# Attention on one core: four column groups of the P·V sums gathered by DMA and added on GpSimd, in place of a closing product on TensorE

## The reference

```python
ctx = X @ We.T
influence = jnp.einsum('bqe,bke->bqk', ctx, ctx)
...
Q, K, V = (heads(Wq), heads(Wk), heads(Wv))
scores = jnp.einsum('bhqd,bhkd->bhqk', Q, K) * SCALE + 0.1 * influence[:, None]
attn = jax.nn.softmax(scores, axis=-1)
out = jnp.einsum('bhqk,bhkd->bhqd', attn, V)
out = out.transpose(0, 2, 1, 3).reshape(b, s, d) @ Wo.T
```

## Time and profile before

| what | value |
|---|---|
| median of 3 runs | 4101.06 us (4098.67 to 4104.31) |
| the profiled execution's own time | 4091.76 us |
| its span, first to last instruction | 4090.0 us |
| mean granted TensorE clock | 0.968 of full speed |
| busy: PE, DVE, ACT, POOL | 93%, 81%, 61%, 12% |
| attention | first product at 483.0 us, last store issued at 3733.3 us of the span |

### The profile page before, as it was taken

How to read it: one execution, slowest core, us unless ns; L and a number is a source line. 1 busy time by engine, 2 the same in 40 slices (tenths; PEclk the granted TensorE clock), 3 DMA queues, 4 the chain that set the end, 5 groups by cost and what they waited for, 6 DMA issues and landing times. The chain is left out here.

```text
span 4090.0 us, 91456 instructions
## 1 busy us (share of the span) xinstructions
PE 3806.7 (93%) x29214; PEld 2212.5 (54%) x29214; DVE 3301.8 (81%) x5171; ACT 2483.3 (61%) x2892; POOL 472.8 (12%) x272
## 2 busy tenths in 40 slices
PE   1997599999999999999999999999999999995698
PEld 1786445555554555555555555555555555553587
DVE  7995488888888888788888888888888888885797
ACT  2663256666666666666666666666666666663464
POOL 3882100000000000000000000000000000000487
PEclk6998799999999999999999999999999999997899
DMA  3002611212122122212121212121212121213200
GB/s 122 1 0 84 160 35 36 44 37 45 36 47 41 41 40 42 44 36 44 36 44 38 44 39 44 38 44 36 44 36 45 38 45 37 47 38 92 69 18 20
DMA packets 316656, 186.52 MB, mean 46 GB/s; under 512 B 195447, under 2 KB 246551, under 8 KB 315831
## 3 DMA queue, kind: packets, MB, share of 16 engines
q1 hardware_dynamic: 316342, 182.35, 20.1%
HBM read 147.75 MB, written 33.82 MB: 44 GB/s over the span
## 5 line engine op out<-in xcount | busy, mean ns | idle before, releaser
L1164 DVE TENSOR_REDUCE tops<-coarse 128x1 f32<-128x512 f32 x4144 | 2681.3, 686 | 578.6 <-PE coarse L1025 475.2
L1140 ACT ACTIVATE probs<-fine 128x1024 f32<-128x1024 f32 x2048 | 1998.5, 1022 | 1014.9 <-PE fine L1044 1014.8
L1055 PE MATMUL o_ps<-probs,vh 128*32 128x512 f32 x8192 | 1088.9, 604 | 0.2 <-ACT probs L1140 0.2
L1034 PE MATMUL fine<-query_a,key_a 64*128 64x512 f32 x4096 | 921.1, 446 | 23.1 <-issue 19.6
L1034 PEld LDWEIGHTS fine<-query_a,key_a 64*128 64x128 f32 x4096 | 386.4, 185 | 929.1 <-ACT probs L1140 750.6
L1025 PE MATMUL coarse<-key_a,max_query 64*128 64x512 f32 x4144 | 832.6, 397 | 43.2 <-DMA key_c<-scratch_c_key 22.3
L1044 PE MATMUL fine<-query_b,key_b 33*128 33x512 f32 x4096 | 816.5, 394 | 0.0
L1040 PE MATMUL fine<-query_c,key_c 64*128 64x512 f32 x4096 | 814.5, 393 | 0.0
L1025 PEld LDWEIGHTS coarse<-key_a,max_query 64*128 64x128 f32 x4144 | 394.2, 186 | 113.5 <-DVE tops L1164 30.0
L1044 PEld LDWEIGHTS fine<-query_b,key_b 33*128 33x128 f32 x4096 | 388.9, 185 | 88.8
L1040 PEld LDWEIGHTS fine<-query_c,key_c 64*128 64x128 f32 x4096 | 389.3, 186 | 82.9
(11 more groups left out here) (158 smaller groups left out, 2377.3 us busy)
## 6 DMA issues: line engine op xcount, KB each, us to landing
query_c<-scratch_c_query SPq DMA_DIRECT2D x258, 128.0 KB, 2.6
max_query<-scratch_q_hi SPq DMA_DIRECT2D x524, 32.0 KB, 1.8
max_query<-scratch_c_query SPq DMA_DIRECT2D x262, 64.0 KB, 2.0
query_a<-scratch_q_hi SPq DMA_DIRECT2D x516, 32.0 KB, 1.8
query_a<-scratch_c_query SPq DMA_DIRECT2D x258, 64.0 KB, 2.0
query_b<-neg_max SPq DMA_DIRECT2D x1032, 0.5 KB, 2.0
query_b<-scratch_q_lo SPq DMA_DIRECT2D x258, 32.0 KB, 2.4
scratch_attended<-result SPq DMA_DIRECT2D x512, 8.0 KB
```

Source lines behind the costliest of these rows:

```text
L1034: pe.matmul(fine[i % 2][:, r, :], key_a[kp][half_rows(r, 0, HALF), cols], query_a[half][half_rows(r, 0, HALF), :], start=True, stop=False)
L1055: last = pe.matmul(o_ps[32 * j:32 * (j + 1), :], vh[kp][:, kt, :], probs[:, kt // 2 % RING, kt % 2, :], start=g == 0, stop=g == NG - 1)
L1140: act.activation(probs[:, i % RING, :, :], fine[i % 2][:, :, :], ACT.Exp).then_inc(probs_ready, 1)
L1164: dve.tensor_reduce(tops[n][:, idx // KB, idx % KB:idx % KB + 1], bank[:, :], AX.X, ALU.max).then_inc(tops_ready, 1)
```

## The change

`finish`, `take_result` and the bank `o_fin` go. ACT copies `o_ps` to one of two `ot` buffers. SP issues four SBUF-to-SBUF DMAs (`gather`) that put the four groups, 17 rows each, side by side on 17 partitions as `part`. POOL adds them in two instructions (`add_parts`): 17 x 1024, then 17 x 512. SP stores `result` with 2 DMAs instead of 5, now behind `load_max`. The ring's skip after unit 23 stays as it is, under the name `SKIP_AFTER`, with nothing in the skipped bank.

```diff
-FINISH_AFTER = 23
+SKIP_AFTER = 23
 SUMS_AFTER = 1
-RESULT_AFTER = 2
...
-        ot = sb("ot", [P, QB])
+        ot = [sb(f"ot{n}", [P, QB]) for n in range(2)]
+        part = [sb(f"part{n}", [DK + 1, QT, QB]) for n in range(2)]
...
-        result = [sb(f"result{n}", [P, P]) for n in range(2)]
+        result = [sb(f"result{n}", [DK + 1, QB]) for n in range(2)]
...
-        o_fin = coarse[(FINISH_AFTER + 1) % COARSE][:, 0:P]
...
+                def add_parts(u, n):
+
+                    pool.wait_ge(gathered[n], G_LEAD + GATHERS * (u + 1))
+                    pool.wait_ge(stored[n], R_LEAD + STORES * u)
+                    pool.tensor_tensor(part[n][:, 0:2, :], part[n][:, 0:2, :], part[n][:, 2:4, :], ALU.add).then_inc(sum_chain, 1)
+                    pool.wait_ge(sum_chain, 2 * u + n + 1)
+                    pool.tensor_tensor(result[n][:, :], part[n][:, 0, :], part[n][:, 1, :], ALU.add).then_inc(result_ready, 1)
...
                 with pool.Fori(0, H // 2 - 1) as hp:
                     for n in range(2):
+                        add_head(2 * hp + n)
 
                         pool.wait_ge(pv_done, V_LEAD + NG * NQB * (2 * hp + n + 1))
                         load_v(n, 2 * hp + n + 2)
...
+                def gather(s, n):
+
+                    sp.wait_ge(ot_ready, O_LEAD + s + 1)
+                    for j in range(QT):
+                        sp.dma_start(part[n][:, j, :], ot[n][32 * j:32 * j + DK + 1, :]).then_inc(gathered[n], 16)
+
                 def store(s, n):
 
-                    sp.wait_ge(result_ready, N_LEAD + s + 1)
+                    sp.wait_ge(result_ready, s + 1)
                     s = (s + STEPS) % STEPS
-                    for j in range(QT):
-                        sp.dma_start(scratch["attended"][bass.ds(s // NQB * DK, DK), bass.ds(s % NQB * QB + j * P, P)],
-                                     result[n][32 * j:32 * j + DK, :]).then_inc(stored[n], 16)
-                    sp.dma_start(scratch["sums"][bass.ds(s // NQB, 1), bass.ds(s % NQB * QB, QB)].rearrange("h (j t) -> (h j) t", j=QT),
-                                 result[n][DK:P:32, :]).then_inc(stored[n], 16)
+                    sp.dma_start(scratch["attended"][bass.ds(s // NQB * DK, DK), bass.ds(s % NQB * QB, QB)], result[n][0:DK, :]).then_inc(stored[n], 16)
+                    sp.dma_start(scratch["sums"][bass.ds(s // NQB, 1), bass.ds(s % NQB * QB, QB)], result[n][DK:DK + 1, :]).then_inc(stored[n], 16)
...
+                                unless_start(half, kp, hp, i, lambda: gather(s - 1, 1 - half))
                                 load_max(s + 1, 1 - half)
+                                unless_start(half, kp, hp, i, lambda: store(s - 1, 1 - half))
...
+                gather(STEPS - 1, 1)
                 store(STEPS - 1, 1)
...
-                        if i == FINISH_AFTER + COARSE:
-                            pe.wait_ge(result_ready, t)
-                        elif not isinstance(t, int) or t > 0 or i >= COARSE:
-                            behind = COARSE if i <= FINISH_AFTER or i > FINISH_AFTER + COARSE else COARSE - 1
+                        if i != SKIP_AFTER + COARSE and (not isinstance(t, int) or t > 0 or i >= COARSE):
+                            behind = COARSE if i <= SKIP_AFTER or i > SKIP_AFTER + COARSE else COARSE - 1
                             pe.wait_ge(tops_ready, UNITS * t + i - behind + 1)
...
-                def finish(s, free):
-
-                    pe.wait_ge(ot_ready, O_LEAD + s + 1)
-                    pe.wait_ge(tops_ready, free)
-                    for j in range(QT):
-                        last = pe.matmul(o_fin[32 * j:32 * (j + 1), :], sel[:, :], ot[:, j * P:(j + 1) * P], start=True, stop=True)
-                    last.then_inc(fin_ready, 1)
...
-                            if unit + 1 == FINISH_AFTER:
-                                before(lambda: finish(s - 1, UNITS * (s + 1) + FINISH_AFTER + 2 - COARSE))
                             times_v(s, kp, i // GROUP - 1)
...
-                def take_sums(s):
+                def take_sums(s, n, earlier):
 
                     act.wait_ge(pv_done, V_LEAD + NG * (s + 1))
-                    act.wait_ge(fin_ready, F_LEAD + s)
-                    act.activation(ot[:, :], o_ps[:, :], ACT.Copy).then_inc(ot_ready, 1)
-
-                def take_result(s, n, earlier):
-
-                    act.wait_ge(fin_ready, F_LEAD + s + 1)
-                    act.wait_ge(stored[n], R_LEAD + STORES * earlier)
-                    act.activation(result[n][:, :], o_fin, ACT.Copy).then_inc(result_ready, 1)
...
+                    act.wait_ge(gathered[n], G_LEAD + GATHERS * earlier)
+                    act.activation(ot[n][:, :], o_ps[:, :], ACT.Copy).then_inc(ot_ready, 1)
```

More of the change, by code:

```diff
@@ L849, in attention_phase @@
         coarse_ready, tops_ready, neg_ready = sem("coarse_ready"), sem("tops_ready"), sem("neg_ready")
-        ot_ready, fin_ready, result_ready = sem("ot_ready"), sem("fin_ready"), sem("result_ready")
+        ot_ready, sum_chain, result_ready = sem("ot_ready"), sem("sum_chain"), sem("result_ready")
+        gathered = [sem(f"gathered{n}") for n in range(2)]
         stored = [sem(f"stored{n}") for n in range(2)]
-        P_LEAD, V_LEAD, F_LEAD, N_LEAD, O_LEAD = 2, RING // GROUP, 1, 1, 1
-        STORES = 16 * (QT + 1)
-        R_LEAD = 2 * STORES
+        P_LEAD, V_LEAD, O_LEAD = 2, RING // GROUP, 1
+        STORES, GATHERS = 16 * 2, 16 * QT
+        R_LEAD, G_LEAD = 2 * STORES, 2 * GATHERS
         C_DMAS, K_DMAS, KB_DMAS, Q_DMAS, MQ_DMAS, M_DMAS = 16 * 6, 16 * 4, 16 * 2, 16 * 10, 16 * 6, 16 * 2 * QT
@@ L890, in load_v, with add_head @@
                     pool.tensor_copy(vh[n][:, :, 0:DK], v_all[:, head, :, :]).then_inc(v_ready, 1)
+                def add_parts(u, n):
[4 more added lines that the diff above has]
+                    pool.tensor_tensor(result[n][:, :], part[n][:, 0, :], part[n][:, 1, :], ALU.add).then_inc(result_ready, 1)
+                def add_head(head):
+                    with pool.Fori(0, NQB // 2) as i:
+                        for n in range(2):
+                            add_parts(head * (NQB // 2) + i, n)
                 load_v(0, 0)
@@ L895, in _ @@
                     for n in range(2):
+                        add_head(2 * hp + n)
                         pool.wait_ge(pv_done, V_LEAD + NG * NQB * (2 * hp + n + 1))
                         load_v(n, 2 * hp + n + 2)
+                for head in range(H - 2, H):
+                    add_head(head)
             @block.sync
@@ L1016, in max_scores @@
                     for i in (idx, idx + 1):
[L1017 to L1020 removed]
+                        if i != SKIP_AFTER + COARSE and (not isinstance(t, int) or t > 0 or i >= COARSE):
+                            behind = COARSE if i <= SKIP_AFTER or i > SKIP_AFTER + COARSE else COARSE - 1
                             pe.wait_ge(tops_ready, UNITS * t + i - behind + 1)
                     for i in (idx, idx + 1):
[L1023 removed]
+                        bank = coarse[(i if i <= SKIP_AFTER else i + 1) % COARSE]
                         q, r, kb = i // KB, i % 2, i % KB // 2
@@ L1142, in body @@
                             if unless_first is None:
-                                take_sums(s - 1)
+                                take_sums(s - 1, 1 - half, u + half - 1)
                             else:
                                 with act.If(unless_first):
-                                    take_sums(s - 1)
-                        if i == RESULT_AFTER:
-                            if unless_first is None:
-                                take_result(s - 1, 1 - half, u + half - 1)
-                            else:
-                                with act.If(unless_first):
-                                    take_result(s - 1, 1 - half, u + half - 1)
+                                    take_sums(s - 1, 1 - half, u + half - 1)
                 steps(act, body)
-                take_sums(STEPS - 1)
-                take_result(STEPS - 1, 1, STEPS // 2 - 1)
+                take_sums(STEPS - 1, 1, STEPS // 2 - 1)
             @block.vector
@@ L1162, in reduce_max @@
                         dve.wait_ge(coarse_ready, UNITS // 2 * t + idx // 2 + 1)
-                    bank = coarse[(idx if idx <= FINISH_AFTER else idx + 1) % COARSE]
+                    bank = coarse[(idx if idx <= SKIP_AFTER else idx + 1) % COARSE]
                     dve.tensor_reduce(tops[n][:, idx // KB, idx % KB:idx % KB + 1], bank[:, :], AX.X, ALU.max).then_inc(tops_ready, 1)
```

18 lines of the change are left out of this document (8 added, 10 removed).

## The result

The changed kernel takes 4113.91 us in the median (4110.38 to 4117.25, 7 runs), the kernel before 4101.06 us (4091.66 to 4104.52, 7 runs). The ratio is 1.0032, 95% interval 1.0020 to 1.0044. The forecast was 4101, range 4085 to 4112. The profiled execution took 4110.38 us with a span of 4108.6 us, 18.6 us longer than that of before. (The profile of before is at the fast end of its runs, 4091.76; the difference of the medians is 12.9.)

What follows compares the result with a forecast made beforehand. PE was taken to set the pace. -6 us in the loop and +5.7 in the tail made 0 within rounding: 4091.5 for the profiled execution, and 4101 with the 9.3 us by which the median lies above it; range 4085 to 4112.

Steps and rivals of the forecast that it cites:

- the wait for unit 23 takes the closing product's place: PE, each step: units 24 and 25 still wait for DVE, so removal gains only 0.047 us, 6 us in all; chance 0.70.
- the product's whole 0.25 us: PE, each step: rival that the wait does not bind, gaining 0.25 us a step, 32 us, to 4075; chance 0.08.
- The load is exposed: PE's weight load for units 24 and 25: no longer hidden, so the product follows 0.34 us after it, not 0.23.
- POOL does not slow DVE's reductions: POOL's adds beside DVE's reductions in the attention: cost taken as 0; the rival, POOL holds DVE, 4470 us, chance 0.04.
- The adds' sum: POOL's two adds a step: 2.43 and 1.21 us, 3.6 us together.
- ACT's lighter load: ACT in the attention: the result's copy goes, worth nothing because ACT waits for PE in most pairs.
- SP's queue: SP's DMAs inside the loop: stores behind load_max push the max_query loads by about 1.2 us, at no cost.
- The tail: Behind the last step: gather, adds and stores without cover take 9.6 us against 3.95, costing 5.7 us, bounds 3.9 and 8.
- lands 2.0 us later: In the tail: the gather's fourth issue begins at about +1.3 us and lands 2.0 us later, at +3.3.
- What is removed on PE: PE without the closing product: it then waits 0.34 us for DVE, gaining 0.047 us a step, 6 us in all.
- longer fetch of code at a loop's end: At a loop's end: a slower outcome given no size, sharing a chance of 0.08 with the longer tail.
- the tail grows: Behind the last step: rival of a 4 us gather or falling clock, 4110 to 4115; 0.08 shared with longer code fetch.

Runs made afterwards that it cites:

- half reductions: Changed kernel with DVE reducing only the first 256 of 512 columns of units 22 and 23: 4085.59 us, ratio 0.9968 to the kernel before.
- the shifts: Changed kernel with 64, 128 or 192 more PE instructions (tiny unused products) once ahead of the attention's first products: 4125.86, 4104.57 and 4105.04 us.
- the 48: Kernel before with 48 more PE instructions (12 tiny products) ahead of the attention's first products, none of the change: 4115.09 us, ratio 1.0040.
- the shift by 128: Changed kernel with 128 more PE instructions (tiny unused products) once ahead of the attention's first products: 4104.57 us, ratio 1.0019 to the kernel before.

## Why the prediction was wrong

**Right.** The step that the wait for unit 23 takes the closing product's place: 0.047 us a step forecast, 0.04 measured (from the early units of the second group to the fourth group's first product 6.00 us, where 6.01 were forecast and 6.06 stood before), the product's whole 0.25 us only with the wait gone (half reductions). The load is exposed, as read from step 0. POOL does not slow DVE's reductions (686 ns). The adds' sum holds, with a little luck, as the first is 0.05 us shorter and the second 0.07 longer than forecast. ACT's lighter load shows no gain: PE's wait accounts for the whole of a step's 0.04 us. SP's queue: later than forecast, since the stores also wait for the adds, but of no cost in a plain step; made as late in the kernel before it cost nothing either.

**The first step that failed: "The tail", its term "lands 2.0 us later".** The mechanism was right, the size was not: 5.7 us forecast, 10.8 measured between marks (10.2 on SP's queue). From the gather's first issue to its use it is 8.34 us for 3.3. With 32 rows it is 3.92, so 4.4 of the 5.0 us are the 17 rows, and 0.6 is the rest, the slower issues among it. I took the landing time from a DMA of another shape, of 0.5 KB, and so missed that the number of rows decides over how many DMA engines a transfer spreads. The Trainium skill ("DMA: Bandwidth & Descriptors", section Why a DMA increments its semaphore by 16 and not by 1) says that a DMA uses the largest number of engines, up to 16, that divides the slowest dimension of both sides; for 17 rows that is one, for 32 it is 16. The measured shares, 0.06 and 0.37, agree with it. This belonged in the forecast.

**The second and larger one: the loop's end, put at nothing.** "What is removed on PE" counted the instructions' time and not their code. Some 200 instructions fewer in the loop moved its end, which made 7 stops 0.8 us longer each (19.6 to 25.4 us) and, in the profiles, let the clock fall at every one: 14.2 us in the profile, 7 to 12 by the medians. That it is the place of the code and not the edit, the shifts show; that it is its place against pieces of 256 instructions is the reading that gave the 48, and no run shows the pieces' borders. I had a "longer fetch of code at a loop's end" at a few per cent with no price; the trace of before has 7 stops of 2.3 to 3.5 us, 19.6 us in all, and would have given one. Its sign could not be read from them: with the same code 128 instructions further on the stops are as before.

The tail's error alone would have stayed within the range (4101 + 5 = 4106), and so would the loop's end by the smaller of its two figures (4101 + 7 = 4108). Together they make 4113, and 4113.91 was measured. The rival "the tail grows", 4110 to 4115, holds the measured time by luck: its reasons were a gather of 4 us or the clock in the output phase, and even a gather of 8.34 us makes only 4106.

Of the clock: in the loop of the shift by 128 it fell for 27 us with stops as short as before. How much of the 14 us is the fetch and how much the clock is only bounded: 5.8 us are longer stops, the other 8.4 lie behind them, slow products among them, and are not split further. What decides whether the clock falls behind a stop of 2.5 us stays open.

## What to carry to other kernels

Before you price a removed instruction, price the wait beside it, and find a place in the trace where the instruction is already absent: here step 0 gave the worth to 0.01 us. A difference of a few tenths of a per cent in a kernel with a long loop can be the layout of its code alone; shift the code by some idle instructions, and look at "issue" behind the loop's end, before you credit or blame an edit. Give a DMA a number of rows that is a multiple of 16, as here 32 for 17, also at the price of rows that nobody reads, and look where in the program a latency has no cover: inside the loop a gather of over 8 us cost nothing (a plain step is 24.72 us with 17 rows and with 32), behind it the stretch shortened by 4.2 us when the gather did by 4.4.

## What the runs showed of the hardware

Twelve idle products ahead of a loop make a kernel of 4098 us 17 us slower, with plain steps and the stretch behind the loop as before (24.76 us and 30.8 to 31.4) and 20 us more at the loop ends in the profile; shifts of the same kind in the changed kernel span 21 us (4104.6 to 4125.9). A DMA of 17 rows of 2 KB keeps one DMA engine of 16 busy (share 0.06), four of them take 8.34 us from the first issue to use, and of 32 rows 3.92 us. A GpSimd add of 17 x 1024 takes 2.38 us, as long for an element of a row as one on 128 partitions (2.32 and 2.37 ns), and leaves a reduction on VectorE that reads PSUM at 686 ns.
